# Latent attention's preparation put in another order, and the turn of the side bank between the maxima

## The chip, the cores and the metric

One core of one Trainium2 chip. The metric is the device time of one execution in microseconds (us); three runs were timed and one more execution was profiled. Engines are called as the profile calls them: PE (TensorE's matmuls), PEld (its weight loads), DVE (VectorE), ACT (ScalarE), POOL (GpSimd), SP (SyncE, which only issues DMAs here).

## The reference

Eight batches of 256 tokens of width 256 go through eight sublayers, in float32, each `x = x + f(layernorm(x))`. The order is latent attention, ternary linear, gated delta attention, ternary linear, latent attention with other weights, and then feed-forward, rotary attention, feed-forward. The change touches the two latent attentions and the closing three sublayers. A latent attention is, cut to what matters:

```python
q  = rmsnorm(x @ Wq_a) @ Wq_b              # 192 wide, to 16 heads of 128 + 64
kv = rmsnorm(x @ Wkv_a) @ Wkv_b            # 64 wide, to 16 heads of keys 128 + values 128
k_rot = rope(x @ Wk_rope); q_rot = rope(q_rot)
p = softmax(where(causal, (q_pass @ k_pass.T + q_rot @ k_rot.T) / sqrt(192), lowest))
o = (p @ v).reshape(B, T, H * 128) @ Wo
```

The ternary linear is `x @ w_ste.T + bias`. Feed-forward and rotary attention both hold a causal attention with 16 heads of width 16; the feed-forward's gate is modulated by `0.1 * tanh(attn @ A) * (h @ A) @ B`.

## The kernel before

Activations of all batches stay in SBUF. The program is a chain of blocks; within a block each engine runs a queue written out by hand, and semaphores order the engines (a `Signal` counts up by a fixed number per batch). Blocks in order: loads, `mla_sublayer` (latent attention, call 0), `delta_sublayer`, `mla_sublayer` (call 1), `small_stream` (the closing three sublayers as one stream).

**The loop of latent attention** (L872 on PE, L925 on VectorE, L973 on ScalarE, L1013 on POOL) runs over 64 pairs of heads, n = 0 to 63, eight pairs (p = 0 to 7) to a batch. In pair n PE does, in this order: scores of both heads of n (L718, L720), the query projection of pair n + 2 (L679, L680), probabilities times values of pair n - 1 (L787, L791), the output projection of pair n - 2 (L811), then a piece of preparation, and the transposes of the probabilities of n (L751, L756). VectorE: the masked maxima of both heads (L186), the scaled product oT of pair n - 2 (L800), which empties the first half of bank 6, the rope products of pair n + 2 (L686, L692), the reciprocal (L770). POOL: the rotary sum of pair n + 2 (L702) and the spread of the reciprocals (L775). ScalarE: exponentials (L739), a copy of queries (L708), copies of transposed probabilities (L765). PE's L787 of pair n - 1 waits for VectorE's oT of pair n - 2.

**The preparation** of the next batch is laid between: statistics of the layer norm on VectorE at p = 0 and the power on POOL; its normalisation (`ln_normalize_dve`, L172) at p = 1, then four transposes of it on PE (L196, `prep_early_pe`); the latent projection (L612) with ScalarE's copies and sums of squares (L629 to L635) at p = 2 and 3; at p = 4 `prep_rms_dve` (L557, L560), `prep_latent_pool` (L581 to L594: the rotary products of the keys, then the inverse rms, which needs ms_eps of L560) and `prep_norm_dve` (L568, L571: the norms of both tiles of 128 tokens); at p = 5 `prep_late_pe` (L643 to L650, six transposes; the last two wait for ScalarE's copy of the first four), `prep_late_act` and `prep_late_dve` (values, L665). The ternary sublayer of another batch goes through the same pieces at p = 5 (statistics), 6 (normalisation L172, transposes L196) and 7 (projection L449, addition L458), in thirteen of the sixteen batches. The last batch of a call has no preparation.

**The closing stream** runs over 96 slots of four heads. In slot s PE does scores (L2336), probabilities times values of s - 1 into bank 7 (L2389, L2393), feed-forward projections (L2461), a side job in bank 7 (token transposes L196, query and key projections L2204, or values L2181), the transposes of the probabilities (L2363), then L2469 and L2501. VectorE: eight masked maxima, two for each of the four heads (L186, `max_dve`), then `oT_dve`: the turn of bank 7 (L2404), reciprocal, scaling, and in every second slot the second turn (L2419). The side job may write bank 7 only when it is turned; the modulation (L2438) at a batch's first slot waits for L2419.

## Time and profile before

| | us |
|---|---|
| median of three runs | 3618.64 |
| lowest, highest | 3610.35, 3619.70 |
| the profiled execution | 3609.97 |
| its span, first to last instruction | 3608.2 |
| PE busy, DVE busy, ACT busy, POOL busy | 3313.0, 2425.1, 1959.2, 817.1 |
| granted TensorE clock, mean of the span | 0.957 |

The profiled execution is 0.24% below the median and next to the lowest run. A busy time is the union of an engine's instructions; PE's includes matmuls that run at the lower clock level, so a low granted clock hides as busy time. The page gives the busy share in 40 slices of the span; latent attention is in slices 1 to 6 and 24 to 29, the stream in the last eleven.

### The profile page before, as it was taken

The numbers are of one execution on the slowest core, as the hardware profiler recorded it, in microseconds if no ns is written. First come the engines' busy times: TensorE is split into PE (matmuls) and PEld (weight loads), VectorE is DVE, ScalarE is ACT, GpSimd is POOL, SyncE is SP. The second block draws the span as 40 slices with busy tenths as digits, with TensorE's granted clock in tenths as the row PEclk, the third lists the DMA queues.
The fourth block names the chain that finished last, engine by engine and source line by source line (L and its number), as shares of the span: only waits on it lengthen the run. The fifth ranks groups of instructions, "written<-read, shape, count | busy, mean of one in ns | idle before, by whom it ended". The sixth has DMA issues, their size and how long they took to land. (4 is left out here: it accounts for less than half of the span.)

```text
span 3608.2 us, 89141 instructions
## 1 busy us (share of the span) xinstructions
PE 3313.0 (92%) x34218; PEld 2701.3 (75%) x34218; DVE 2425.1 (67%) x7923; ACT 1959.2 (54%) x4767; POOL 817.1 (23%) x827
## 2 busy tenths in 40 slices
PE   6888896999999999999999868888979999999999
PEld 5676774888888888888888756766757777777787
DVE  4665654778777777777777535565656767777764
ACT  2444453666666666666666524454545555555553
POOL 2322221222222222222222222222210111111100
PEclk8998997999999999999999978898989999999999
DMA  5000000000000000000000040000000000000000
GB/s 223 1 1 1 1 1 18 14 20 20 20 20 20 20 20 20 20 20 20 20 20 20 8 151 1 1 1 1 1 1 1 1 1 1 1 1 7 4 7 10
DMA packets 51336, 66.83 MB, mean 19 GB/s; under 512 B 4962, under 2 KB 40290, under 8 KB 49378
## 3 DMA queue, kind: packets, MB, share of 16 engines
q1 hardware_dynamic: 50914, 61.13, 5.3%
q8 instruction: 274, 4.49, 0.5%
q14 instruction: 148, 1.21, 0.1%
HBM read 58.56 MB, written 2.56 MB: 17 GB/s over the span
## 5 line engine op out<-in xcount | busy, mean ns | idle before, releaser
L1286 DVE SCALAR_TENSOR_TENSOR d_acc<-d_raw,d_taps,d_acc 128x255 f32<-128x255 f32 (+2 forms) x1152 | 642.9, 599 | 146.2 <-ACT d_raw L1276 132.6
L2355 ACT ACTIVATE s_probs<-s_probs,s_nmax 128x128 f32<-128x128 f32 (+1 forms) x768 | 280.7, 443 | 187.9 <-DVE s_nmax L186 187.3
L1511 ACT COPY d_power<-bank 128x768 f32<-128x768 f32 x320 | 259.0, 809 | 218.7 <-PE bank L1504 218.7
L702 POOL TENSOR_TENSOR a_q<-a_rope 64x512 f32<-64x512 f32 x128 | 164.0, 1281 | 738.7 <-DVE a_rope L692 384.7
L186 DVE CUSTOM_DVE_ANT_0 a_area<-bank,mask 128x128 f32<-128x128 f32 (+1 forms) x512 | 160.3, 355 | 241.8 <-PE bank L720 239.4
L739 ACT ACTIVATE a_area<-a_area,a_nmax 128x128 f32<-128x128 f32 (+1 forms) x512 | 226.6, 444 | 165.2 <-DVE a_nmax L186 164.1
L1274 ACT ACTIVATE d_acc<-bank,d_tap_bias,d_taps 128x256 f32<-128x256 f32 x384 | 196.0, 561 | 166.5 <-PE bank L1255 158.7
L186 DVE CUSTOM_DVE_ANT_0 s_probs<-bank,mask 128x128 f32<-128x128 f32 (+1 forms) x768 | 220.9, 353 | 61.7 <-PE bank L2336 60.6
L765 ACT COPY a_area<-bank 128x512 f32<-128x512 f32 (+1 forms) x260 | 140.1, 578 | 138.7 <-PE bank L756 138.1
L2377 DVE COPY s_probsT<-bank 128x384 f32<-128x384 f32 x192 | 106.0, 555 | 119.9 <-PE bank L2363 117.7
L692 DVE TENSOR_TENSOR a_rope<-bank,a_sinT 32x512 f32<-32x512 f32 x256 | 177.4, 693 | 5.6
L720 PE MATMUL bank<-a_latT,a_q 128*128 128x256 f32 x512 | 172.2, 422 | 0.0
L1314 POOL TENSOR_TENSOR d_qT<-d_acc,d_sigm 128x512 f32<-128x512 f32 x64 | 84.4, 1319 | 370.5 <-ACT d_sigm L1296 370.5
L679 PE MATMUL bank<-a_latT,a_wq 128*128 128x256 f32 x512 | 154.8, 384 | 7.9 <-DVE a_rope L692 4.5
L1654 POOL TENSOR_TENSOR d_o_rs<-d_o_var,minus_half 128x4 f32<-128x4 f32 x64 | 69.5, 1087 | 402.4 <-DVE d_o_var L1648 402.4
L811 PE MATMUL bank<-a_w_out,a_area 128*128 128x256 f32 x512 | 154.3, 426 | 1.9 <-DVE a_area L800 1.9
L680 PE MATMUL bank<-a_qT,a_wq 128*128 128x256 f32 x512 | 153.1, 381 | 0.0
L2363 PE MATMUL bank<-ident,s_probs 128*128 128x128 f32 x1152 | 147.9, 276 | 4.6 <-ACT s_probs L2355 1.8
L686 DVE TENSOR_TENSOR a_rope<-bank,a_cosT 64x512 f32<-64x512 f32 x128 | 88.9, 695 | 92.3 <-PE bank L680 91.8
L2363 PEld LDWEIGHTS bank<-ident,s_probs 128*128 128x128 f32 x1152 | 131.7, 142 | 19.0 <-ACT s_probs L2355 11.3
L2461 PE MATMUL bank<-s_xT,m_w_up 128*128 128x256 f32 x512 | 140.5, 397 | 4.1 <-DVE s_hidden L2492 4.1
L180 POOL TENSOR_TENSOR rstd<-var_eps,minus_half 128x2 f32<-128x2 f32 x64 | 46.0, 718 | 432.8 <-DVE var_eps L162 428.0
(267 smaller groups left out, 8783.3 us busy)
## 6 DMA issues: line engine op xcount, KB each, us to landing
d_alpha<-d_alpha_rows SPq DMA_DIRECT2D x64, 256.0 KB, 3.5
d_g_decay<-d_running_rows SPq DMA_DIRECT2D x32, 258.0 KB, 3.4
a_w_o<-in_a_w_o SPq DMA_DIRECT2D x2, 2048.0 KB, 16.5
a_area<-in_a_q_nope SPq DMA_DIRECT2D x2, 1536.0 KB, 8.2
x<-in_x SPq DMA_DIRECT2D x8, 256.0 KB, 16.3
d_wk<-in_d_wk SPq DMA_DIRECT2D x1, 2048.0 KB
d_wq<-in_d_wq SPq DMA_DIRECT2D x1, 2048.0 KB
d_wv<-in_d_wv SPq DMA_DIRECT2D x1, 2048.0 KB
```

Of the source, the lines that this page charges most:

```text
L186: return core.nc.vector.tensor_tensor_reduce(out=out, in0=scores, in1=core.mask[:, blocks], scale=-1.0, scalar=HIGHEST, op0=ALU.add, op1=A ...
L679: nc.tensor.matmul(out, wq0[:, h], latT[:, it % 2, 0], start=True, stop=False)
L692: last = nc.vector.tensor_tensor(rope2[other], b_q[rows, :].rearrange("p (j t) -> p j t", j=2), sinT[rows].rearrange("p (j t) -> p j t", j ...
L702: nc.gpsimd.tensor_tensor(q[CL:P, n % 2], rope1[CL:P], rope2[CL:P], ALU.add)\
L720: nc.tensor.matmul(out[:, P:3 * P], q[:, n % 2, j, P:T], keys, start=False, stop=True, skip_group_check=True).then_inc(g.scores_in_psum.se ...
L739: last = nc.scalar.activation(own, own, ACT.Exp, scale=-1.0, bias=nmax[:, h % AHEAD, t:t + 1], accum_out=sums[:, n % 2, j, t:t + 1])
L811: last = nc.tensor.matmul(b_y[:, t * D:(t + 1) * D], oT[:, n % 2, t * P:(t + 1) * P], w_out[:, p], start=(p == 0 and t == 0), stop=(p == P ...
L1274: nc.scalar.activation(acc[:, r % 3, j], b_proj[:, j * T:(j + 1) * T], ACT.Identity, scale=taps[:, r // 2, h, 3:4], bias=tap_bias[:, r // ...
L1286: last = nc.vector.scalar_tensor_tensor(out=acc[:, r % 3, j, d:T], in0=raw[:, r % 2, j, 0:T - d], scalar=taps[:, r // 2, h, 3 - d:4 - d], ...
L1511: nc.scalar.copy(power[:], b_step[:, :, 0:3 * P]).then_inc(g.step_out, 1)
L2355: last = nc.scalar.activation(own, own, ACT.Exp, scale=-1.0, bias=nmax[:, s % 2, t, i:i + 1])
L2363: last = nc.tensor.transpose(heads[:, i, n * P:(n + 1) * P], probs[:, s % 2, i, n * P:(n + 1) * P], core.ident[:])
```

## The change

In `mla_sublayer`: the last two transposes of `prep_late_pe` go to the unused half of bank 6 (`b_qT1`), so they don't wait for ScalarE's copy; the norms are split by tile, tile 0 at the end of pair 4 and tile 1 in pair 5 before the values copy; `prep_rms_dve` and the late part stand ahead of the rope; the normalisations at p = 1 and p = 6 stand right behind the maxima, ahead of oT; on POOL the latent part at p = 4 stands ahead of the rotary sum of pair n + 2, which now also waits for the inverse rms. In `small_stream`: the turn (`turn_dve`) is taken out of `oT_dve` and stands between the maxima of heads one and two and of three and four. No instruction is added or removed. The diff:

```diff
--- before.py
+++ after.py
@@ -385,6 +385,7 @@
         b_prep, b_q, b_s, b_pT, b_o, b_y = (core.bank[0], core.bank[1], core.bank[3:5],
                                             [core.bank[5], core.bank[2]], core.bank[6],
                                             core.bank[7])
+        b_qT1 = b_o[0:QL1, T:2 * T]
         PAIRS_ALL = NB * PAIRS
 
 
@@ -560,11 +561,12 @@
             nc.vector.tensor_scalar(ms_eps[:], ms[:], 1e-6, None, ALU.add)\
                 .then_inc(g.ms_eps_ready.sem, 1)
 
-        def prep_norm_dve(dve, it):
-            dve.wait_ge(*g.rms_ready(it, 1))
-            dve.wait_ge(*g.latT_in_psum(it, 0))
-            dve.wait_ge(*g.v_ready(it, 0))
-            for t in range(NT):
+        def prep_norm_dve(dve, it, tiles):
+            for t in tiles:
+                if t == 0:
+                    dve.wait_ge(*g.rms_ready(it, 1))
+                    dve.wait_ge(*g.latT_in_psum(it, 0))
+                    dve.wait_ge(*g.v_ready(it, 0))
                 nc.vector.scalar_tensor_tensor(
                     out=q_tok[:, t], in0=lat[:, t, 0:QL], scalar=inv_rms[:, t, 0:1],
                     in1=norm_w[:, 0:QL], op0=ALU.mult, op1=ALU.mult).then_inc(g.norm_ready.sem, 1)
@@ -639,14 +641,14 @@
             pe.wait_ge(*g.norm_ready(it, 2 * NT))
             pe.wait_ge(*g.kpe_ready(it, 1))
             pe.wait_ge(*g.lat_ready(it, NT))
+            pe.wait_ge(*g.latT_ready(it, 0))
             for t in range(NT):
                 nc.tensor.transpose(b_prep[:, t * P:(t + 1) * P], q_tok[:, t, 0:P], core.ident[:])
                 last = nc.tensor.transpose(b_prep[:, T + t * P:T + (t + 1) * P], k_tok[:, t],
                                            core.ident[:])
             last.then_inc(g.latT_in_psum.sem, 1)
-            pe.wait_ge(*g.latT_ready(it, 1))
             for t in range(NT):
-                last = nc.tensor.transpose(b_prep[0:QL1, t * P:(t + 1) * P], q_tok[:, t, P:QL],
+                last = nc.tensor.transpose(b_qT1[:, t * P:(t + 1) * P], q_tok[:, t, P:QL],
                                            core.ident[:])
             last.then_inc(g.latT_in_psum.sem, 1)
 
@@ -657,7 +659,7 @@
             nc.scalar.copy(latT[:, half].rearrange("p a t -> p (a t)"), b_prep[:, :])\
                 .then_inc(g.latT_ready.sem, 1)
             act.wait_ge(*g.latT_in_psum(it, 2))
-            nc.scalar.copy(qT1[0:QL1, half], b_prep[0:QL1, 0:T]).then_inc(g.latT_ready.sem, 1)
+            nc.scalar.copy(qT1[0:QL1, half], b_qT1).then_inc(g.latT_ready.sem, 1)
 
         def prep_late_dve(dve, it):
             dve.wait_ge(*g.norm_ready(it, 2 * NT))
@@ -910,7 +912,7 @@
                 if after_attention:
                     ternary_row_sum_dve(dve)
                 prep_rms_dve(dve, -1)
-                prep_norm_dve(dve, -1)
+                prep_norm_dve(dve, -1, range(NT))
                 prep_late_dve(dve, -1)
                 if after_attention:
                     ternary_weight_dve(dve)
@@ -927,28 +929,30 @@
                     if n < PAIRS_ALL:
                         max_dve(dve, n, 0)
                         max_dve(dve, n, 1)
+                    if it + 1 < NB and p == 1:
+                        ln_normalize_dve(core, dve, mla_at(it + 1), it + 1)
+                    if ternary_in(it) is not None and p == 6:
+                        ln_normalize_dve(core, dve, ternary_at(ternary_in(it)), ternary_in(it))
                     if n > 1:
                         oT_dve(dve, n - 2)
+                    if it + 1 < NB:
+                        if p == 4:
+                            prep_rms_dve(dve, it)
+                        if p == 5:
+                            prep_norm_dve(dve, it, [1])
+                            prep_late_dve(dve, it)
                     if n + 2 < PAIRS_ALL:
                         rope_dve(dve, n + 2)
+                    if n < PAIRS_ALL:
+                        recip_dve(dve, n)
                     if it + 1 < NB:
                         if p == 0:
                             mla_stats_dve(dve, it + 1)
-                        if p == 1:
-                            ln_normalize_dve(core, dve, mla_at(it + 1), it + 1)
                         if p == 4:
-                            prep_rms_dve(dve, it)
-                        if p == 5:
-                            prep_late_dve(dve, it)
-                    if n < PAIRS_ALL:
-                        recip_dve(dve, n)
-                    if it + 1 < NB and p == 4:
-                        prep_norm_dve(dve, it)
+                            prep_norm_dve(dve, it, [0])
                     if ternary_in(it) is not None:
                         if p == 5:
                             ternary_stats_dve(dve, ternary_in(it))
-                        if p == 6:
-                            ln_normalize_dve(core, dve, ternary_at(ternary_in(it)), ternary_in(it))
                         if p == 7:
                             ternary_add_dve(dve, ternary_in(it))
                     if n > 1 and p == 1:
@@ -1013,14 +1017,14 @@
                 for n in range(PAIRS_ALL):
                     it, p = n // PAIRS, n % PAIRS
                     pool.wait_ge(*g.q_rope_ready(0, min(n + 2, PAIRS_ALL)))
+                    if it + 1 < NB and p == 4:
+                        prep_latent_pool(pool, it)
+                        pool.wait_ge(*g.rms_ready(it, 1))
                     if n + 2 < PAIRS_ALL:
                         rope_pool(pool, n + 2)
                         pool.wait_ge(*g.q_rope_ready(0, n + 3))
-                    if it + 1 < NB:
-                        if p == 0:
-                            ln_rstd_pool(core, pool, mla_at(it + 1))
-                        if p == 4:
-                            prep_latent_pool(pool, it)
+                    if it + 1 < NB and p == 0:
+                        ln_rstd_pool(core, pool, mla_at(it + 1))
                     if ternary_in(it) is not None:
                         if p == 5:
                             ln_rstd_pool(core, pool, ternary_at(ternary_in(it)))
@@ -2339,10 +2343,10 @@
                                             skip_group_check=True)
             last.then_inc(g.scores_in_psum, 1)
 
-        def max_dve(dve, s):
+        def max_dve(dve, s, members_):
             need(dve, g.scores_in_psum, s + 1)
             need(dve, g.probsT_in_psum, GS * (s - 1))
-            for i in range(GS):
+            for i in members_:
                 for t, cols in ((0, slice(0, P)), (1, slice(P, 3 * P))):
                     masked_max_dve(core, probs[:, s % 2, i, cols], heads[:, i, cols], cols,
                                    nmax[:, s % 2, t, i:i + 1]).then_inc(g.max_ready, 1)
@@ -2395,13 +2399,15 @@
                                         tile_position=(0, 32 * i), skip_group_check=True)
             last.then_inc(g.pv_in_psum, 1)
 
-        def oT_dve(dve, s):
-
-            j, k = s // SETS, s % SETS
-            cols = slice(HD * (k % 2), HD * (k % 2 + 1))
+        def turn_dve(dve, s):
             need(dve, g.pv_in_psum, s + 1)
             need(dve, g.scaled, s)
             nc.vector.transpose(turned[:], b_side[:, 0:T]).then_inc(g.turned, 1)
+
+        def oT_dve(dve, s):
+
+            j, k = s // SETS, s % SETS
+            cols = slice(HD * (k % 2), HD * (k % 2 + 1))
             need(dve, g.turned, s + 1)
             nc.vector.reciprocal(recip[:], blocks(turned[:])[:, :, HD:HD + 1])\
                 .then_inc(g.recip_ready, 1)
@@ -2571,7 +2577,11 @@
                     for i, step in steps_at(s - 1):
                         hidden_dve(dve, i, step)
                     if 0 <= s < SLOTS:
-                        max_dve(dve, s)
+                        max_dve(dve, s, range(GS // 2))
+                    if 0 < s <= SLOTS:
+                        turn_dve(dve, s - 1)
+                    if 0 <= s < SLOTS:
+                        max_dve(dve, s, range(GS // 2, GS))
                     if k == 0 and is_ffn(j + 1):
                         var2_dve(dve, j + 1)
                     if 0 < s <= SLOTS:
```

## Rows read from the trace of the kernel before

**Rows 1.** Windows, loops and stream: busy us of PE, PEld, DVE, ACT, POOL; clock; DMA.
```profile
54.57:552.27 497.70, 435.46 (x2446) 349.39 (x2444) 301.71 (x991) 245.28 (x790) 140.17 (x181) 0.92 0.02 6
2133.05:2637.67 504.62, 443.61 (x2442) 355.62 (x2440) 298.55 (x983) 246.96 (x790) 138.74 (x180) 0.91 0.00 1
2672.65:3608.17 935.52, 887.64 (x6861) 697.50 (x6860) 635.50 (x2637) 506.54 (x1360) 94.85 (x91) 0.99 0.01 4
```
**Rows 2.** Waits of PE, first call's loop: us in total, times, longest.
```profile
PE bank L196 <- DVE xn L172: 29.5, 13, 4.2
PE bank L787 <- DVE a_area L800: 26.8, 8, 3.6
```
**Rows 3.** Windows: fourth batch by pair, p = 1 to 7; last, another batch's pair 7.
```profile
247.71:256.58 8.87, 6.80 (x42) 5.44 (x41) 7.22 (x23) 4.21 (x13) 3.89 (x5) 0.96 0.00 0
256.58:264.94 8.36, 8.36 (x41) 6.50 (x41) 3.88 (x13) 3.73 (x13) 1.38 (x2) 0.84 0.01 2
264.94:272.01 7.07, 7.07 (x43) 5.48 (x41) 3.88 (x13) 4.52 (x17) 1.67 (x3) 1.00 0.00 0
272.01:277.78 5.77, 5.77 (x38) 4.71 (x37) 4.05 (x15) 4.05 (x16) 0.44 (x2) 1.00 0.00 0
277.78:291.83 14.05, 9.75 (x45) 7.58 (x43) 6.37 (x25) 4.70 (x14) 6.28 (x10) 0.69 0.01 1
291.83:302.05 10.22, 8.08 (x42) 6.60 (x42) 5.45 (x15) 4.13 (x12) 2.98 (x3) 0.83 0.00 1
302.05:310.31 8.26, 8.26 (x45) 6.86 (x45) 4.55 (x14) 3.20 (x11) 1.66 (x2) 0.91 0.00 1
169.88:177.38 7.50, 7.50 (x47) 6.23 (x46) 4.56 (x14) 3.46 (x12) 1.98 (x3) 1.00 0.00 0
```
**Rows 4.** Timeline (start, us, instruction, idle before), VectorE and PE behind scores at 264.94.
```profile
265.80 0.29 DVE L186 CUSTOM_DVE_ANT_0 a_area<-bank,mask 128x128 f32<-128x128 f32 x1 [2.35 <-PE bank L720]
...
267.02 0.42 DVE L800 TENSOR_TENSOR a_area<-bank,a_area 128x256 f32<-128x256 f32 x1
...
268.08 0.44 PE L787 MATMUL bank<-a_area,a_values 128*64 128x256 f32 x2
268.18 0.69 DVE L686 TENSOR_TENSOR a_rope<-bank,a_cosT 64x512 f32<-64x512 f32 x1 [0.75 <-PE bank L680]
```
**Rows 5.** Timeline, end of pair 4 and pair 5: POOL's chain and VectorE.
```profile
277.40 0.16 DVE L557 TENSOR_TENSOR a_ms<-a_sumsq,a_ms_scale 128x4 f32<-128x4 f32 x1
...
278.98 0.45 POOL L581 TENSOR_TENSOR a_k_t<-a_lat,a_cos_tok 128x128 f32<-128x128 f32 x1
...
281.43 0.20 POOL L594 TENSOR_TENSOR a_inv_rms<-a_inv_rms,a_q_scale 128x4 f32<-128x4 f32 x1
281.67 0.51 DVE L568 SCALAR_TENSOR_TENSOR a_q_tok<-a_lat,a_inv_rms,a_norm_w 128x192 f32<-128x192 f32 x1 [3.81 <-POOL a_inv_rms L594]
...
282.92 0.29 DVE L186 CUSTOM_DVE_ANT_0 a_area<-bank,mask 128x128 f32<-128x128 f32 x1
```
**Rows 6.** Timeline: normalisation beside POOL at p = 1, and in the stream.
```profile
253.11 1.68 DVE L172 TENSOR_SCALAR xn<-x,mean_var,rstd 128x256 f32<-128x256 f32 x2
253.33 1.31 POOL L702 TENSOR_TENSOR a_q<-a_rope 64x512 f32<-64x512 f32 x1 [3.28 <-DVE a_rope L692]
...
2925.08 0.73 DVE L172 TENSOR_SCALAR xn<-x,mean_var,rstd 128x256 f32<-128x256 f32 x2
```
**Rows 7.** Closing stream: costliest groups of the page, timeline, and a wait of PE.
```profile
L2355 ACT ACTIVATE s_probs<-s_probs,s_nmax 128x128 f32<-128x128 f32 (+1 forms) x768 | 280.7, 443 | 187.9 <-DVE s_nmax L186 187.3
L186 DVE CUSTOM_DVE_ANT_0 s_probs<-bank,mask 128x128 f32<-128x128 f32 (+1 forms) x768 | 220.9, 353 | 61.7 <-PE bank L2336 60.6
...
2901.69 0.40 PE L2393 MATMUL bank<-s_probsT,s_v 128*32 128x128 f32 x8
2903.60 0.45 DVE L2404 STREAM_TRANSPOSE s_turned<-bank 128x256 f32<-128x256 f32 x1
...
PE bank L196 <- DVE s_turned L2404: 10.7, 8, 2.0
```

More of the change, by code:

```diff
@@ L2396, in pv_pe @@
             last.then_inc(g.pv_in_psum, 1)
+        def turn_dve(dve, s):
+            need(dve, g.pv_in_psum, s + 1)
+            need(dve, g.scaled, s)
+            nc.vector.transpose(turned[:], b_side[:, 0:T]).then_inc(g.turned, 1)
         def oT_dve(dve, s):
@@ L2401, in oT_dve @@
             cols = slice(HD * (k % 2), HD * (k % 2 + 1))
-            need(dve, g.pv_in_psum, s + 1)
-            need(dve, g.scaled, s)
-            nc.vector.transpose(turned[:], b_side[:, 0:T]).then_inc(g.turned, 1)
             need(dve, g.turned, s + 1)
```

## The prediction

> **What bounds the kernel now.** I first read the busy time of the stages that the change touches [rows 1]; delta attention between them stays as it is. In the two calls of latent attention (64 head pairs each) PE is busy 435 of 498 us and 444 of 505 us, and its granted clock is only 0.92 and 0.91: some 60 us idle in each, and besides that work done at the lower of the two clock levels (1.2 instead of 2.4 GHz). In the closing stream it is 888 of 936 us at 0.99. So PE is the bound in all three, and the only time to be had is where PE stands still or runs slow.
>
> Who stops it is in the waits of PE in the first call [rows 2]: 29.5 us in its transposes of the normalised tokens (L196, for VectorE's L172) and 26.8 us before probabilities times values (L787, for VectorE's L800). Where in a batch this lies shows when one batch is cut at the first scores matmul of each pair [rows 3]. An ordinary pair (p = 4) takes 5.77 us with PE busy for all of it. Pairs 2 and 3 carry the latent projection: 7.07 at full clock. Pair 7 carries the ternary projection: 7.50 at full clock. Pair 1 takes 8.87 with 2.07 idle, pair 5 takes 14.05 with 4.3 idle and clock 0.69, pair 6 takes 10.22 with 2.1 idle and clock 0.83; and pairs 2 and 7, which don't idle, take 8.36 and 8.26 since the clock is still low behind the stall before them (0.84, 0.91). All the excess is in and behind pairs 1, 5 and 6, the three that the change rearranges.
>
> **Pair 5, the large stall.** Before, VectorE ends pair 4 with prep_norm_dve and sits 3.81 us for POOL's inverse rms; POOL starts its latent products (L581) only at 278.98, when the rotary sum of pair 6 is out of its way, and needs until 281.63 [rows 5]. The maxima of pair 5 stand behind that wait, the output product (L800) behind the maxima, and PE behind L800. Pair 5's scores began at 277.78, so by the ordinary pair [rows 4] its maxima were due at 278.64 (0.86 after its scores) and came at 282.92.
> After, POOL does the latent part first in pair 4. It is free early: ScalarE makes the second latent tile in pair 3, ahead of that pair's transposed copies, so by pair 4's scores at 272.01, and the whole chain from L581 to the end of L594 is 2.65 us long [rows 5]. Its middle waits for ms_eps, which VectorE now makes ahead of the rope: the ordinary pair leaves VectorE 0.75 us idle there [rows 4], and the two small instructions (the first takes 0.16 [rows 5]) need some 0.35, so they cost nothing (without that cover, 0.35 x 14 = 5 us). They come behind L800, 2.5 us after pair 4's scores, from 274.5 to 274.85. Were the whole chain behind them, inv_rms would be there at 277.5; the three latent products don't need ms_eps, so I take 276.3. The rope of pair 6 ends on VectorE at 277.4, so neither POOL's rotary sum, now queued behind the wait for rms, nor the norm waits. What stood in the stall is gone.
> What is late next: tile 0's two norms lie between 277.5 and 278.6; four norms took 1.25 us, from 281.67 to 282.92 [rows 5], so two take 0.63. The second meets POOL's rotary sum (1.31 us) and may be held by it, as the second normalisation is in [rows 6]; then it ends at about 279.1 and the maxima of pair 5 are 0.45 late. L787 starts 3.14 after the scores and L800 is done 2.50 after them [rows 4], some 0.5 us of slack with the signal's way, so 0.45 still fits. Tile 1's norms (0.63) and the values copy (0.3, an estimate from the norms) follow L800, which leaves 0.74 free before the rope, and push the rope of pair 7 by up to 0.6 us; nobody needs that rope for more than a pair. PE then has six transposes more than an ordinary pair. Eight matmuls of 256 columns make pair 7 longer by 7.50 - 5.77 = 1.73 [rows 3], 0.216 each, so a transpose of 128 columns is 0.11 and six are 0.65; their wait for ScalarE in between is gone because the second group goes to the free half of bank 6. Pair 5: 5.77 + 0.65 = 6.42.
>
> **Pairs 1 and 6, the normalisation.** Before, it comes behind the rope, takes 1.68 us for two instructions and meets POOL's rotary sum, which runs from 253.33; in the closing stream the same two take 0.73 with POOL idle [rows 6]. So the second is held until POOL is through (254.64; it ends at 254.79). After, it stands right behind the maxima, where POOL has nothing but the last 0.1 us of a spread to do: I take 0.75 to 0.9 us.
> The Trainium skill (SBUF — State Buffer, Who interferes with whom) has this as a rule: a VectorE instruction in a 2-port mode, or one with two SBUF inputs against a POOL instruction that reads SBUF, takes the shared port pair exclusively, and who starts first blocks the other. By that rule the normalisation is freed, and the second norm of tile 0 is held in its place; the trace agrees in [rows 6]. Were POOL no matter, the two would cost 1.68 wherever they stand, and the time would be that of the rival "held" below.
> The price is that L800 and the rope move back by that time. Of the 0.75 to 0.9 the slack of 0.5 before L787 takes most; with VectorE 0.2 to 0.4 late into both pairs (pair 0's statistics, pair 5's tail) a PE stall of 0.55 in pair 1 and 0.5 in pair 6 is left in place of 2.07 and 2.1. With four transposes (0.43): pair 1 6.75, pair 6 6.70. Bounds of the stall: 0 (everything in the slack) and 1.5 (the instructions still held). VectorE's own work in pair 1 was 7.22 us [rows 3], of which 1.68 - 0.73 = 0.95 was being held: 6.3, still under PE's 6.75, but near.
>
> **The clock.** The short stalls decide whether the clock falls too. In the batch shown it is 0.96 and then 0.84 around the 2.07 us stall of pair 1, 0.69 in pair 5, and 1.00 in pairs without a stall [rows 3]. The closing stream keeps 0.99 although PE waits 8 times for the turn, 1.3 us each on average [rows 1, 7]. I take the clock as full for the whole loop after the change, for pairs 2 and 7 too.
>
> **The sum for latent attention.** A batch with a ternary step: 5.77 + 6.75 + 7.07 + 7.07 + 5.77 + 6.42 + 6.70 + 7.50 = 53.05. Each call has six of these, one without the ternary step (pairs 6 and 7 at 5.77: 50.39), and the last batch, which prepares nothing and has seven periods up to the window's end, 7 x 5.77 and at most one ternary normalisation: 41. Together 409.7 us. Before, the two windows are 497.70 and 504.62 [rows 1]. Saved: 88.0 + 94.9 = 182.9 us. The preparation ahead of each loop loses one short wait of PE between two groups of transposes, beside the weights' staging; bounded by the 2.07 us of the longer wait in pair 1 it is 0 to -4 for both calls, and I take 0.
>
> **The closing stream.** The turn (L2404, 0.45 us) now comes after four of eight maxima, 1.15 us sooner: 220.9 us of maxima in 96 slots are 2.30 a slot, half of it 1.15. It needs the product of values, whose last matmuls (L2393) end at 2902.09, while half of the maxima are done at 2903.60 - 1.15 = 2902.45 [rows 7]; so in an ordinary slot it does not wait. In 8 slots PE waited for the turn with the token transposes (L196), 10.7 us [rows 7], of which at most 1.15 each can go, less where PE then meets the last head's exponentials: about 0.85 x 8 = 7. A few other projections wait for the same signal; they are in the bound. The wait of the modulation (L2438) for `oT` stays: that chain still ends behind all eight maxima. Heads three and four get their maxima 0.45 later, but ScalarE needs 280.7/384 = 0.73 us a head against VectorE's 0.58 and is behind by then, so 0.1 us reaches the exponentials; most slots give PE other work there. Net -7; bounds -11 and +10 (0.1 in each of 96 slots).
>
> Sum: 3609.97 (the profiled execution; span 3608.2) - 182.9 - 7 = 3420. The median of the runs is 3618.64, the fastest 3610.35, so the profile stands at the low end. I give **3420**.
>
> **Rivals.**
> Clock: the remaining half-microsecond stalls still make the clock fall. Price from [rows 3]: pair 1 without a fall would be 5.77 + 0.43 + 2.07 = 8.27 and took 8.87, pair 2 took 8.36 for 7.07; 1.9 us in all, for 14 pairs 1 and 12 pairs 6: 49 us, 3469. For it: 2.07 was enough. Against: the stream. Chance 0.14.
> Held: POOL still runs beside the normalisation, which keeps its 1.68 and stalls PE 0.95 more, 26 times: 25 us, 3445. For it: POOL's spread or power can slip there when VectorE enters the pair late. Against: both are shorter than the rotary sum. Chance 0.10.
> Half: the order in pair 4 doesn't do what it says: ms_eps or the latent tile comes so late that POOL's rotary sum and tile 0 wait for it, and half the gain of the loops is lost, 3420 + 91 = 3511. It decides if inv_rms is later than 277.5, 1.2 us after my estimate. Chance 0.04.
> Slower: the turn in the middle of the maxima waits for the values' product and puts its 0.45 us into the path of every slot, 96 x 0.45 = 43 us, while in the loops the stall only moves from L568 to the rope's consumers: 3610 + 43 = 3653. It decides from the point where the loops give back under 43 of 183 us. For it: VectorE does the same work in the same time. Against: 0.4 us between the product's end and the turn. Chance 0.02.
> My forecast has 0.69, the last 0.01 is for no change. Its own spread is 3400 (no stalls left, stream at -11) to 3440. The range takes in the clock rival: 3395 to 3470. A measurement can tell 0.3%, 11 us. Faster by over that 0.97, within 0.01, slower 0.02.
>
> **What would show it.** Cut at the first scores matmul, pair 5 near 6.4, pairs 1 and 6 near 6.7, pairs 2 and 7 at 7.07 and 7.50, granted clock near 1.00 in both loops; the wait of L568 for POOL gone; L787's wait for L800 left with many entries of half a microsecond; L172 at 0.75 to 0.9 for two. In the stream, L196's waits for the turn (10.7 us) down to some 4 us, L2438's for `oT` as before. Wrong would be: clock under 0.97 in the loops, POOL's rotary sum of pair 6 starting over 0.5 us behind the rope, or exponentials turning up among PE's waits in the stream.

## The result, and the profile after

The changed kernel takes **3391.14 us** (median of four runs, 3390.88 to 3391.84); the kernel before, timed with it, 3618.28 (3610.35 to 3619.70). The ratio is 0.9377, with a 95% interval from 0.9361 to 0.9393: 6.2% faster. The forecast was 3420, the range 3395 to 3470. The direction and the size of the large part (the loops) were right, and the time lies 29 us below the forecast and 4 below the range.

The profiled execution took 3391.38 us with a span of 3389.6, against 3609.97 and 3608.2 before. From the top of the profile's page, the busy time of each engine and the granted clock in 40 slices:

```profile
PE 3221.4 (95%) x34218; PEld 2645.8 (78%) x34218; DVE 2403.6 (71%) x7923; ACT 1954.6 (58%) x4767; POOL 820.5 (24%) x827
...
PEclk8999989999999999999999979999989999999999
```

PE is busy 92 us less with the same 34218 instructions (3313.0 before); the mean granted clock went from 0.957 to 0.980. The windows of the two loops of latent attention and of the stream, answering to [rows 1] (us, busy us of PE, PEld, DVE, ACT, POOL, clock, DMA share, GB/s):

```profile
51.99:458.36 406.37, 399.61 (x2446) 324.83 (x2445) 295.59 (x991) 239.90 (x790) 141.96 (x182) 1.00 0.03 10
2034.91:2439.71 404.80, 399.16 (x2442) 324.41 (x2441) 293.48 (x983) 240.78 (x790) 140.07 (x180) 1.00 0.01 1
2474.84:3389.60 914.76, 878.60 (x6861) 699.14 (x6860) 625.08 (x2637) 512.51 (x1360) 94.95 (x91) 1.00 0.01 4
```

The loops gave 91.3 and 99.8 us, 191.1 together (forecast 182.9). The stream gave 20.8 (forecast 7, bound 11). The three stretches outside them gave 2.6 (up to the first scores), 4.2 (between the calls) and nothing (0.1 the other way) before the stream. That is the whole difference of 218.6.

One batch, cut at the first scores matmul of each pair from p = 0 to 7, answering to [rows 3]:

```profile
259.35:265.12 5.77, 5.77 (x38) 4.71 (x37) 4.10 (x15) 3.40 (x12) 0.15 (x1) 1.00 0.01 3
265.12:271.70 6.58, 6.28 (x42) 5.24 (x41) 6.20 (x22) 3.84 (x13) 2.99 (x4) 1.00 0.00 0
271.70:278.77 7.07, 7.07 (x43) 5.48 (x41) 3.88 (x13) 3.79 (x13) 2.25 (x4) 1.00 0.00 0
278.77:285.83 7.06, 7.06 (x42) 5.47 (x41) 3.88 (x13) 4.50 (x17) 1.67 (x3) 1.00 0.01 2
285.83:291.61 5.78, 5.78 (x39) 4.72 (x38) 4.33 (x16) 4.06 (x16) 3.03 (x7) 1.00 0.01 1
291.61:298.04 6.43, 6.43 (x45) 5.37 (x44) 6.26 (x20) 4.06 (x14) 1.98 (x3) 1.00 0.00 0
298.04:304.42 6.38, 6.27 (x42) 5.23 (x41) 5.31 (x20) 3.92 (x13) 2.74 (x4) 1.00 0.00 0
304.42:311.93 7.51, 7.51 (x47) 6.25 (x46) 4.56 (x14) 3.47 (x12) 3.79 (x5) 1.00 0.02 4
```

PE stands still only in pairs 1 and 6, 0.30 and 0.11 us, and the clock is full in all eight. Pair 5 fell from 14.05 to 6.43 us. In the timeline of its VectorE and POOL (start, duration, instruction, idle before and releaser) the chain that was the stall now lies inside pair 4, which began at 285.83:

```profile
288.43 0.17 DVE L561 TENSOR_SCALAR a_ms_eps<-a_ms 128x4 f32<-128x4 f32 x1
...
291.32 0.39 DVE L570 SCALAR_TENSOR_TENSOR a_q_tok<-a_lat,a_inv_rms,a_norm_w 128x192 f32<-128x192 f32 x1
291.63 1.30 DVE L573 SCALAR_TENSOR_TENSOR a_k_tok<-a_lat,a_inv_rms,a_norm_w 128x64 f32<-128x64 f32 x1
292.96 0.29 DVE L186 CUSTOM_DVE_ANT_0 a_area<-bank,mask 128x128 f32<-128x128 f32 x1
...
294.74 0.28 DVE L573 SCALAR_TENSOR_TENSOR a_k_tok<-a_lat,a_inv_rms,a_norm_w 128x64 f32<-128x64 f32 x1
```

```profile
286.21 0.46 POOL L583 TENSOR_TENSOR a_k_t<-a_lat,a_cos_tok 128x128 f32<-128x128 f32 x1
...
289.78 0.20 POOL L596 TENSOR_TENSOR a_inv_rms<-a_inv_rms,a_q_scale 128x4 f32<-128x4 f32 x1
291.43 1.42 POOL L704 TENSOR_TENSOR a_q<-a_rope 64x512 f32<-64x512 f32 x1 [1.45 <-DVE a_recip L772]
```

POOL starts the latent products 0.38 us after the scores of pair 4 and has the inverse rms at 289.98, long before VectorE asks for it at 291.32. The second norm of tile 0 (L573 at 291.63) takes 1.30 us beside POOL's rotary sum and 0.28 alone, for tile 1 at 294.74. The maxima of pair 5 begin 1.35 us after its scores, 0.49 late against the 0.86 of an ordinary pair [rows 4], and PE loses nothing by it.

### The profile page after: what moved, and what is told of

It is laid out like the page before. It is cut to its first block and busy times, and to the rows that moved or that the text cites. A ratio compares the mean times of both kernels' runs of the same rounds, so it can differ in the third digit from the quotient of the medians.

```text
span 3389.6 us, 89251 instructions
## 1 busy us (share of the span) xinstructions
PE 3221.4 (95%) x34218; PEld 2645.8 (78%) x34218; DVE 2403.6 (71%) x7923; ACT 1954.6 (58%) x4767; POOL 820.5 (24%) x827
## 5 line engine op out<-in xcount | busy, mean ns | idle before, releaser
L2359 ACT ACTIVATE s_probs<-s_probs,s_nmax 128x128 f32<-128x128 f32 (+1 forms) x768 | 287.9, 447 | 184.4 <-DVE s_nmax L186 183.6
L2367 PE MATMUL bank<-ident,s_probs 128*128 128x128 f32 x1152 | 148.4, 275 | 6.3 <-ACT s_probs L2359 3.6
L722 PE MATMUL bank<-a_latT,a_q 128*128 128x256 f32 x512 | 152.9, 380 | 0.0
L2367 PEld LDWEIGHTS bank<-ident,s_probs 128*128 128x128 f32 x1152 | 130.5, 141 | 21.9 <-ACT s_probs L2359 14.4
L813 PE MATMUL bank<-a_w_out,a_area 128*128 128x256 f32 x512 | 144.7, 405 | 1.9 <-DVE a_area L802 1.9
L1508 PE MATMUL bank<-d_power 64*64 64x64 f32 x4096 | 142.2, 217 | 0.0
```

The costliest lines, as they stand in the source:

```text
L722: nc.tensor.matmul(out[:, P:3 * P], q[:, n % 2, j, P:T], keys, start=False, stop=True, skip_group_check=True).then_inc(g.scores_in_psum.se ...
L2359: last = nc.scalar.activation(own, own, ACT.Exp, scale=-1.0, bias=nmax[:, s % 2, t, i:i + 1])
L2367: last = nc.tensor.transpose(heads[:, i, n * P:(n + 1) * P], probs[:, s % 2, i, n * P:(n + 1) * P], core.ident[:])
```

## What was held against what

The stream had given three times its term. The first expectations hold two readings of that against each other. **M** is the forecast's own: only the time in which PE's matmuls stood still for the turn can be won, 7 to 11 us, and the rest of what was gained comes out of the latent part. **W** was formed after the result, from the trace of the kernel before: in 32 more slots only PE's weight load came late for the turn, without a gap between the matmuls, and each of these hides some 0.35 us. A third reading is that the stream gains by a state which the loops leave behind, the phase of the clock or of the queues. The other questions were how the loops' gain divides (H, in these expectations, is the forecast's account that POOL's rotary sum holds the second instruction of the normalisation), and what the turn's place does to the two other users of VectorE in a slot, the exponentials and the modulation.

The runs were made in three series, 1 to 4, 5 to 8 and 9 to 12, on three chips, each with the kernel before beside them (3616.20, 3618.00 and 3617.94 us). Unless said otherwise, a median is compared with the changed kernel's 3389.61 us in the second series, or with the kernel before in the same series.

## Experiments

**1. The stream's change alone, on the kernel before.** Only `turn_dve` is taken out of `oT_dve`:

```diff
-                        max_dve(dve, s)
+                        max_dve(dve, s, range(GS // 2))
+                    if 0 < s <= SLOTS:
+                        turn_dve(dve, s - 1)
+                    if 0 <= s < SLOTS:
+                        max_dve(dve, s, range(GS // 2, GS))
```

> The kernel before with the split of the turn alone. Theory W (hidden weight loads): in the trace of before PE's weight loads wait for the turn 32.9 us in 42 slots, while its matmuls wait only 13.2 us in 10; the other 32 slots hide some 0.35 us each, because the first weight load after the wait no longer overlaps the matmul in front of it. So the stream gets shorter by 20 to 21 us (935.5 to about 915) and the time with it. Rival M (matmul gaps alone, as predicted): 7 to 11 us, and the rest of what the changed kernel gained came out of the latent part. Everything ahead of the stream as before within 1 us or a step of the clock.

3594.09 us (3586.04 to 3595.05), ratio 0.9929 [0.9915, 0.9944], 22 us less; in its profile the stream takes 912.6 instead of 935.5. The whole of the stream's gain comes from the turn, with the loops as they were. M with its 7 to 11 us is out, and so is a state left by the loops. The profile also shows how much the loops scatter by themselves: the first takes 505.5 us here and 497.7 in the kernel before, with the same code.

**2. The loops' change alone**: the changed kernel with the stream's edit undone.

> The changed kernel without the split of the turn: only the latent attention's part. Theory W: 3391 + 20.5 = 3412, the two loops at 406.4 and 404.8 us as in the changed kernel, the stream at 935. Rival M: 3391 + 7 to 11 = 3398 to 3402.

3415.90 us (3408.59 to 3416.83), ratio 0.9437 [0.9423, 0.9451]; loops 406.3 and 404.9, stream 935.9. 200 us here and 22 there are 222, and both together gave 227 (first comparison) and 228 (second series): they add up within the scatter.

**3. The normalisation back behind the rope**, all else as changed:

```diff
-                    if it + 1 < NB and p == 1:
-                        ln_normalize_dve(core, dve, mla_at(it + 1), it + 1)
-                    if ternary_in(it) is not None and p == 6:
-                        ln_normalize_dve(core, dve, ternary_at(ternary_in(it)), ternary_in(it))
                     if n > 1:
                         oT_dve(dve, n - 2)
...
                         rope_dve(dve, n + 2)
+                    if it + 1 < NB and p == 1:
+                        ln_normalize_dve(core, dve, mla_at(it + 1), it + 1)
                     if n < PAIRS_ALL:
                         recip_dve(dve, n)
+                    if ternary_in(it) is not None and p == 6:
+                        ln_normalize_dve(core, dve, ternary_at(ternary_in(it)), ternary_in(it))
```

> The changed kernel with the normalisations of pairs 1 and 6 put back behind the rope. Theory H (the second of the two instructions is held by POOL's rotary sum): both take 1.68 us again for two, PE waits 2.07 us in 26 pairs, and a pair 1 without a fall of the clock takes 8.5 (6.58 now): 26 x 1.9 = 50 us; with the clock falling behind each of them, 3.4 each: 88 us. I expect 3445 to 3480, with granted clock under 0.97 in the loops. Rival: with the large stall of pair 5 gone, PE's short stalls are absorbed and it costs under 25 us.

3471.01 us (3469.07 to 3476.76), ratio 0.9598 [0.9582, 0.9614]; some 80 us more than the changed kernel, loops 446.9 and 443.2. PE waits 87.8 us in 31 for L172 again, as in the kernel before. A pair 1 with the pair 2 behind it, as windows:

```profile
287.45:297.03 9.58, 7.50 (x42) 6.15 (x41) 7.15 (x22) 4.34 (x13) 3.90 (x5) 0.88 0.00 0
297.03:304.69 7.66, 7.66 (x42) 5.98 (x42) 3.89 (x13) 3.48 (x12) 1.38 (x2) 0.92 0.00 0
```

The stall of 2.1 us is back, and with it the fall of the clock (0.88, 0.92) in or behind 11 of the 14 pairs 1, but only 4 of the 12 pairs 6 with the same stall. This also gives a number that the forecast lacked: where the clock doesn't fall, pair 1 with its stall takes 8.50 us (calculated there as 8.27).

**4. POOL's latent part back behind the rotary sum**, all else as changed:

```diff
-                    if it + 1 < NB and p == 4:
-                        prep_latent_pool(pool, it)
-                        pool.wait_ge(*g.rms_ready(it, 1))
                     if n + 2 < PAIRS_ALL:
                         rope_pool(pool, n + 2)
                         pool.wait_ge(*g.q_rope_ready(0, n + 3))
+                    if it + 1 < NB and p == 4:
+                        prep_latent_pool(pool, it)
```

> The changed kernel with POOL's latent part put back behind the rotary sum of pair 6. Theory: VectorE's norm of tile 0 waits for POOL until 4 us behind the rope's end again, pair 5 goes from 6.43 to 12 or 13 us and pair 6 gets a lower clock: 14 x (6 + 1.5) = 105 us, 3490 to 3505. Rival (the split of the norms by tile and the early ms_eps do most of it): under 50 us.

3451.51 us (3449.84 to 3452.95), ratio 0.9540 [0.9526, 0.9554]: 62 us more, neither the 100 to 115 of the theory nor the under 50 of its rival. Pair 5 takes 9.6 to 12.6 us, most often 11.3. A pair 5 and the pair 6 behind it:

```profile
308.78:320.06 11.28, 8.18 (x45) 6.93 (x44) 6.52 (x24) 4.61 (x14) 5.72 (x9) 0.85 0.00 0
320.06:326.42 6.36, 6.27 (x42) 5.24 (x41) 4.53 (x15) 3.58 (x12) 1.31 (x3) 1.00 0.00 0
```

The stall is there, but shorter (PE busy 8.18 of 11.28, so 3.1 us idle for 4.3 in before), and the clock is back inside pair 5 (0.85, in before 0.69), and pair 6 pays nothing (6.36 at full clock, in before 10.22). My expectation had carried the clock's price of before [rows 3] over into a kernel that pays it less. Run 11 finds part of where it went.

**5. The changed kernel again**, as the reference of its series.

> The changed kernel itself, on the same chip as the next three, to compare them with. 3391 us, loops 406.4 and 404.8, stream 914.8.

3389.61 us (3388.60 to 3395.88), ratio 0.9369 [0.9357, 0.9382]; loops 406.3 and 404.8, stream 914.6.

**6. The normalisation one place later**, between the scaled product and the rope:

```diff
+                    if n > 1:
+                        oT_dve(dve, n - 2)
                     if it + 1 < NB and p == 1:
                         ln_normalize_dve(core, dve, mla_at(it + 1), it + 1)
                     if ternary_in(it) is not None and p == 6:
                         ln_normalize_dve(core, dve, ternary_at(ternary_in(it)), ternary_in(it))
-                    if n > 1:
-                        oT_dve(dve, n - 2)
```

> The changed kernel with the normalisations of pairs 1 and 6 between the scaled product and the rope, not ahead of the product. Theory H: it is free of POOL there too (0.73 to 0.8 us for two), and PE's wait in front of the values' product (12.1 us in 19 times) goes; pair 1 6.58 to about 6.25, pair 6 6.39 to 6.22: 13 x 0.33 + 13 x 0.18 = 6.6 us, 3384.5. Rival: the rope is 0.8 late there and POOL's rotary sum with it, which gives the gain back or more: 3391 or above.

3380.30 us (3379.76 to 3380.85), ratio 0.9340 [0.9327, 0.9353]. The loops take 402.3 and 401.4. A pair 1:

```profile
263.16:269.37 6.21, 6.21 (x43) 5.15 (x42) 5.96 (x22) 3.84 (x13) 2.62 (x4) 1.00 0.00 0
```

PE is busy throughout, and pairs 1 and 6 take 6.21 in place of 6.58 and 6.38. What the change left there was L802 coming late for L789, and it costs 0.37 and 0.17 us a pair, of which 0.30 and 0.11 were idle time of PE. The normalisation stays free of POOL here too (L172 at most 413 ns). The normalisation can wait that long: its transposes lie behind the projections of the same pair.

**7. The turn after three heads** (six of eight maxima) instead of two:

```diff
-                        max_dve(dve, s, range(GS // 2))
+                        max_dve(dve, s, range(3))
...
-                        max_dve(dve, s, range(GS // 2, GS))
+                        max_dve(dve, s, range(3, GS))
```

> The changed kernel with the turn behind the maxima of three heads instead of two, so 0.56 us later. Theory W: half of the hidden weight-load waits are back, the weight loads' wait for the turn is between 6.6 us (changed) and 32.9 (before), and the stream is 8 to 12 us longer: 923 to 927, 3400. Rival M: under 4 us.

3393.07 us (3391.06 to 3396.86), ratio 0.9377 [0.9364, 0.9389]; stream 913.4. I expected half of the gain to go, and little went. The stream's 913.4 against 914.6 flatters it: in run 5 the clock is low in slots 0 and 76 (0.76 and 0.85) and here it is full, which is worth 3.1 us. The slots in which PE's matmuls wait for the turn are 2.3 us longer together (L196's waits grow from 2.9 to 6.3 us), and all other slots 0.4 shorter, so the edit costs some 2 us. But of the 32 slots in which only the weight load had waited 30 are as short as in run 5. So their gain is not in proportion to the advance: they need the turn only some 0.35 us sooner, and 0.58 does that as well as 1.15.

**8. The whole chain up to oT between heads two and three, in the slots with k = 0**:

```diff
                         turn_dve(dve, s - 1)
+                        if k == 0:
+                            oT_dve(dve, s - 1)
...
-                    if 0 < s <= SLOTS:
+                    if 0 < s <= SLOTS and k > 0:
                         oT_dve(dve, s - 1)
```

> The changed kernel with the whole chain to oT (turn, reciprocal, scaling, second turn) between heads two and three in each item's first slot, where the modulation waits for it. Theory: that wait (L2444 for L2425, 13.4 us in 9 times) falls by the 1.15 us of the four maxima each, 9 to 10 us; the exponentials of heads three and four are 1 us later but PE has the modulation's matmuls meanwhile: 3381 to 3384. Rival: the transposes of the probabilities then wait for the last heads and take it back: 3388 to 3392.

3379.68 us (3377.39 to 3384.31), ratio 0.9341 [0.9328, 0.9354]; stream 904.9, 9.7 less. The wait of the modulation, 13.4 us in nine before this edit:

```profile
  PE bank L2444: 3.7, 5
```

What the change had left of that chain behind all maxima is worth some 8 us by its slots. That the stream lost 9.7, as much as the wait, is in part luck: eight of the nine slots with the modulation are 1.0 us shorter, slot 76 is 2.5 shorter because the clock doesn't fall in it either, and slot 48, where no modulation waits, is 1.0 longer.

**9. Both better places together** (6 and 8):

> The changed kernel with both other placements at once: the normalisation between the scaled product and the rope, and the whole chain of the turn up to oT between heads two and three in the slots with k = 0. Alone they took 9.3 and 9.9 us off. They lie in different stages, so the theory expects the sum: 3389.6 - 19 = 3370 (3367 to 3374), loops of 402.3 and 401.4 us, stream near 905. Rival: part of one gain was the phase of the clock between the stages, and the two together give under 14 us (over 3375).

3374.15 us (3373.30 to 3379.85), ratio 0.9334 [0.9320, 0.9349]. Where the edits lie, both gains are there in full:

```profile
52.19:454.58 402.39, 399.53 (x2445) 324.43 (x2444) 295.54 (x991) 239.94 (x790) 141.70 (x182) 1.00 0.03 11
2036.39:2437.75 401.36, 398.33 (x2442) 323.36 (x2440) 293.31 (x983) 240.78 (x790) 139.82 (x180) 1.00 0.01 1
2472.86:3378.06 905.20, 877.68 (x6861) 698.24 (x6860) 627.27 (x2637) 514.60 (x1360) 94.86 (x91) 1.00 0.01 4
```

3.9, 3.4 and 9.4 us less than in run 5. The median gave 15 and not 19, a little outside what was expected; by the ratios (0.9334 for 0.9369) it is 13, which would be the rival's side. That the two add up is shown by the windows and not by the times. In this profile the stretch between the calls, which no edit touches, took 1581.8 us and in that of run 5 1573.6; over all profiles here it takes 1573.6 to 1581.8. A difference of 4 us between medians is within that. This is the fastest median of the study, though its interval overlaps those of 6 and 8 alone.

**10. The turn after the first head:**

```diff
-                        max_dve(dve, s, range(GS // 2))
+                        max_dve(dve, s, range(1))
...
-                        max_dve(dve, s, range(GS // 2, GS))
+                        max_dve(dve, s, range(1, GS))
```

> The changed kernel with the turn after the first head's maxima. It is asked for 0.58 us earlier still; by the row of the product of values (end 2902.09 in the slot shown, first head's maxima done at 2901.87) it then waits some 0.2 us for the product in an ordinary slot. Theory (only the first projections of a slot care, and nearly all are already free): stream within 3 us of 914.6, at most 4 of the 9.2 + 5.3 us of weight-load waits go, time 3386 to 3392. Rival, the mechanism of the forecast's case slower: the wait of the turn stands in the path of three heads' maxima in 96 slots, 0.2 x 96 = 19 us, stream near 930, time over 3400, exponentials among PE's waits.

3396.89 us (3394.22 to 3398.53), ratio 0.9393 [0.9379, 0.9407]; stream 920.4, 5.8 longer than in run 5 and in neither case's band. The turn waits for the product of values, but 3.7 us in 7 slots and not in all 96. The price stands where the exponentials are waited for. Who waited for L2359, the exponentials' line, with the turn after three, two and one heads, one line from each kernel (us, times):

```profile
  PEld bank L2367: 11.5, 26
```

```profile
  PEld bank L2367: 14.3, 32
```

```profile
  PEld bank L2367: 23.1, 52
```

With the turn behind all four heads it is 11.3 us in 26. Every head whose maxima stand behind the turn gets its exponentials 0.45 us later. After one head ScalarE has no backlog yet (it stands still for the maxima 162 times here and 89 in run 5), the delay reaches PE's transposes and outweighs what the turn still gives. The stream takes 935.9 us with the turn behind all four heads, 913.4 behind three (3.1 of it clock, as said), 914.6 behind two and 920.4 behind one: behind two or three it makes little difference.

**11. Bank 6 alone, on the kernel before:** the second group of transposes goes to the free half of bank 6 and no longer waits for ScalarE's copy.

```diff
-            pe.wait_ge(*g.latT_ready(it, 1))
             for t in range(NT):
-                last = nc.tensor.transpose(b_prep[0:QL1, t * P:(t + 1) * P], q_tok[:, t, P:QL],
+                last = nc.tensor.transpose(b_qT1[:, t * P:(t + 1) * P], q_tok[:, t, P:QL],
```

> The kernel before with the second group of transposes (L649) in the free half of bank 6 and nothing else. In before PE and its weight loads wait 27.7 us in 32 entries for ScalarE's copy L657, two entries to each of 16 preparations, so some 0.87 us a preparation of PE's path, 12 us for the 14 that lie in the loops. Theory: faster than before by 10 to 14 us, call loops near 492 and 499. Rival: in pair 5 VectorE's late chain is the later one anyway (the wait of L787 grows by what L649 loses) and under 4 us come.

3565.81 us (3562.49 to 3569.93), ratio 0.9858 [0.9841, 0.9875]: **52 us**, where I had worked out 10 to 14. In the profiles, whose kernel before stands at the low end of its runs, it is 40: 37.8 in the loops and 2.6 up to the first scores (45.5 in the loops against run 1's profile, which has the loops of before as well). Pairs 5, 6 and 7 of a batch in the kernel before, and the same batch here:

```profile
346.16:360.20 14.04, 9.74 (x44) 7.56 (x43) 6.35 (x25) 4.70 (x14) 6.26 (x10) 0.69 0.00 0
360.20:370.42 10.22, 8.08 (x41) 6.59 (x41) 5.46 (x15) 4.08 (x12) 2.98 (x3) 0.83 0.01 3
370.42:378.63 8.21, 8.21 (x45) 6.82 (x45) 4.55 (x14) 3.15 (x11) 1.67 (x2) 0.91 0.00 0
```

```profile
336.56:349.44 12.88, 9.26 (x44) 7.44 (x43) 6.36 (x25) 4.34 (x14) 6.27 (x10) 0.73 0.00 0
349.44:358.01 8.57, 6.43 (x43) 5.07 (x41) 5.46 (x15) 3.79 (x13) 2.66 (x3) 1.00 0.00 1
358.01:365.51 7.50, 7.50 (x47) 6.23 (x45) 4.55 (x14) 3.46 (x12) 1.99 (x3) 1.00 0.01 3
```

The large stall is untouched. In pair 5 the wait for the copy (0.68 us) goes and 1.16 comes; but 1.65 comes in pair 6 and 0.71 in pair 7, where nothing was edited: the clock is back before pair 6 begins, and the stall of pair 6 (2.1 us, in both) is not followed by a low clock. This batch is one of those with the largest gains. Over the 14 batches of both loops pair 5 gives 11.7 us (as much as I had worked out), pair 6 14.8, pair 7 8.1 and the others 3.2: some two thirds of the worth of this edit lie outside pair 5, and since PE's idle time there is the same, they are clock. It is also part of why undoing POOL's order in run 4 cost less than the theory said: there the second transposes no longer wait, and the stall of pair 5 is 3.1 us, where it is 3.6 here and 4.3 in before.

**12. All four norms together** at the end of pair 4, in the changed kernel:

```diff
                         if p == 5:
-                            prep_norm_dve(dve, it, [1])
                             prep_late_dve(dve, it)
...
-                            prep_norm_dve(dve, it, [0])
+                            prep_norm_dve(dve, it, range(NT))
```

> The changed kernel with all four norms together at the end of pair 4 (tile 1's two no longer behind the scaled product of pair 5). Theory of the forecast: the maxima of pair 5 come 0.56 us later than now (two norms of 0.28), on top of 0.45, against a slack of 0.5 before the product of values: PE stalls 0.5 us more in pair 5, pair 5 at 6.9 instead of 6.43, 14 x 0.5 = 7 us slower than the changed kernel, 3396 (3393 to 3400). Rivals: the slack takes it all (within 2 us, pair 5 at 6.4), or the stall makes the clock fall (pair 5 over 7.5, over 3405).

3394.24 us (3393.79 to 3395.41), ratio 0.9387 [0.9373, 0.9401], 4.6 us more than the changed kernel; loops 410.1 and 408.5, 7.5 us more than in run 5. A pair 5:

```profile
293.66:300.66 7.00, 6.50 (x45) 5.46 (x43) 6.79 (x23) 4.06 (x14) 2.74 (x3) 1.00 0.00 0
```

7.00 against 6.43: the slack of half a microsecond ahead of L789 is real and ends where the forecast had it end, and a stall of 0.50 us leaves the clock at 1.00.

## Why the forecast was right where it was, and where it failed

**The step that failed: the stream's term.** The forecast put -7 with a bound of -11, and the stream gave 20.8. That is 14 of the 29 us by which the time was missed. The loops gave 8 more than their sum and the stretches outside 7 where 0 was put (see below); since the time is only 4 us below the range, either of these two, had it come out as forecast, would have kept it inside as well. But they are misses of size, and the stream's is one of mechanism. With -21 in the stream's place the sum would have been 3406, and a range moved with it by the same 14 us (3381 to 3456) would have held the time. The turn was asked for 1.15 us sooner, as said, and the waits of L196 fell from 10.7 to 2.9 us, as said (to some 4). The mistake was in the count: "in 8 slots PE waited for the turn", and the bound was built on those 8. Only the matmuls' waits had been read. Who waited for the turn, L2404 in the kernel before, weight loads (PEld) included (us, times):

```profile
  PEld bank L2438: 18.0, 9
  PEld bank L196: 15.9, 12
  PE bank L196: 10.7, 8
  PEld bank L2204: 9.3, 19
  PEld bank L2181: 7.7, 11
  PE bank L2181: 2.5, 2
```

The same for L2405 in the changed kernel:

```profile
  PEld bank L2444: 9.2, 4
  PEld bank L196: 5.3, 6
  PE bank L196: 2.9, 6
  PEld bank L2185: 1.1, 2
```

The weight loads of the three side jobs waited in 12 + 19 + 11 = 42 slots, their matmuls in 10. In the other 32 the weight load came late behind the turn and the matmul right with it, less than 0.1 us behind the modelled end of the matmul ahead, so that no wait of PE is listed. A slot of before in the timeline, and its like of after (the kernel before first):

```profile
2961.55 1.03 PE L2461 MATMUL bank<-s_xT,m_w_in 128*128 128x256 f32 x4
...
2962.66 1.59 PEld L2181 LDWEIGHTS bank<-m_wv,s_xT 128*128 128x128 f32 x8 [0.49 <-DVE s_turned L2404]
2962.66 1.99 PE L2181 MATMUL bank<-m_wv,s_xT 128*128 128x256 f32 x8
```

```profile
2756.66 1.03 PE L2467 MATMUL bank<-s_xT,m_w_in 128*128 128x256 f32 x4
...
2757.31 1.70 PEld L2185 LDWEIGHTS bank<-m_wv,s_xT 128*128 128x128 f32 x8
2757.53 1.89 PE L2185 MATMUL bank<-m_wv,s_xT 128*128 128x256 f32 x8
```

From the start of one matmul group to the start of the next it is 1.11 us before and 0.87 after, and the second lasts 1.99 and 1.89: 0.34 us in a slot in which no wait of PE is listed.

I matched the 95 slot periods of the two profiles (slots counted from 0) one by one; the piece behind them is the same in both. The 32 slots in which the weight load alone had waited are shorter by 0.30 to 0.41 us, **11.1 us together**: the part that was not seen. The ten in which the matmuls had waited too gave 7.7: 5.5 in the eight of L196, for which 7 was said, and 2.2 in the two of L2181. So what was priced came out near its price and inside the bound. The nine slots with the modulation gave 0.14 each (1.3 together), as their wait for oT fell from 14.7 to 13.4 us. The rest is mostly clock. Slot 28 in the kernel before, with a wait of 1.94 us and the clock at 0.88, and in the changed kernel, with a wait of 1.80 and the clock at 1.00:

```profile
2925.63:2939.99 14.36, 12.42 (x79) 9.76 (x78) 7.95 (x32) 6.17 (x18) 3.12 (x3) 0.88 0.00 1
2723.08:2735.63 12.55, 10.75 (x80) 8.52 (x79) 7.76 (x32) 6.25 (x18) 3.12 (x3) 1.00 0.01 1
```

Slot 44 is the same, and the two gave 3.4 by the clock. Slots 76 and 0, where the clock is lower after than before, took 1.5 and 0.6 back, and the others together 0.6. In run 1, where the clock falls in none of slots 28, 44 and 76, the 32 slots gave the same 11.1. It also shows in the busy time: of the 20.8 us only 11.7 were idle time of PE (47.9 to 36.2, from [rows 1] and the window above), 9.0 went out of "busy", 8.3 of them in the 32 slots. The Trainium skill (Perfetto Trace Analysis, Tensor Engine Instruction (MATMUL, LD_WEIGHTS)) says that a matmul's end in the profile is estimated rather than observed and that PE can pull weight loads ahead of matmuls in flight; this case's rows agree: after, the weight load starts at 2757.31, 0.38 us before the modelled end of the matmuls ahead. PE's gaps alone were for that reason no bound. That it is a threshold and not proportional is run 7, and that the order of the maxima has a price is run 10.

**Heads three and four 0.45 us later** was costed at 0.1 or less a slot and hidden in most. Right in size: the matmuls' waits for the exponentials grow from 1.8 us in 2 (L2363) to 3.6 in 9 (L2367) in the whole stream, and those of the weight loads, which must be read too, from 11.3 in 26 to 14.4 in 32. The bound of +10 was never near with the turn in the middle; run 10 shows where it begins.

**Pair 5** came out at 6.43 for 6.42. Its steps too: ms_eps done 2.8 us after the scores (2.8), inverse rms 4.15 after them (4.29), the second norm of tile 0 held by POOL's rotary sum, the maxima 0.49 late (0.45), nothing lost on PE. Run 12 takes the slack away and gets the stall.

**Pairs 1 and 6** were put at 6.75 and 6.70 and take 6.58 and 6.38: the stalls left cost 0.37 and 0.17 (run 6) where 0.55 and 0.5 had been said, since VectorE enters both pairs less late than assumed. L172 is freed altogether. Its durations over the whole kernel, minimum, median and maximum in ns, in the changed kernel (before, the maximum was 1357):

```profile
L172 DVE TENSOR_SCALAR xn<-x,mean_var,rstd x128: 400/408/466, 10.8 to 3270.4; 128x256 f32<-128x256 f32 x128
```

With that, the rule of the Trainium skill weighed in the forecast (SBUF — State Buffer, Who interferes with whom) held in both directions: the instruction that no longer meets POOL is short (0.47 us at most), and the norm that now meets it is held to 1.30 us. The rival "held" is out.

**The clock** was taken as full in the loops, and it is: 1.00 in every pair. The clock rival rested on pair 1's 2.07 us being enough for a fall. The stalls left inside the batches are 0.1 to 0.4 us (PE idles up to 2.0 in a pair at the two ends of a loop), and no pair shows a lower clock behind them, nor behind the 0.50 of run 12. The loops gave 8.2 us more than the sum: 0.17 and 0.32 a batch in pairs 1 and 6 make 5 to 6 of it, and the first and last batches, some of which are 1 us shorter than put in, the rest.

**The stretches outside** were taken as 0 with a bound of -4 and gave 6.7. Up to the first scores it is 2.6, and run 11, with bank 6 alone, gives the same 2.6, so it is likely that edit's: the profiles with it have their first scores at 50.5 to 52.3 us, the two without at 54.3 and 54.6. The 4.2 between the calls I can't assign: this stretch takes 1573.6 to 1581.8 us in the kernels that share its code. The forecast put no term for a stretch that is hardly edited, and it moves by up to 8 us between executions.

**What the forecast had wrong without paying for it:** it gave bank 6 no share of its own. Alone it is 52 us; in the changed kernel it may be worth only the short wait, since no stall is left to recover from. That wasn't tried, nor were the early ms_eps and the place of the late part undone by themselves, and which part of the 200 us "belongs" to which edit depends on the order in which they are made: bank 6 first 52; POOL's order last 62; the normalisation last 81; the split by tile last 5 (7.5 by the loops' windows).

## What to carry to other kernels

Where the engine that bounds is PE, read who waited for a signal with its weight loads, not its matmuls alone: a late weight load behind a matmul cost some 0.35 us a time here and left PE "busy". Price a stall with what the clock does behind it: a short wait that lies in the recovery of a long one can be worth four times its length (0.68 us of PE's idle time, 2.7 us a batch in run 11), and perhaps only itself once the long one is gone, which wasn't tried. When a step is moved ahead on a full engine, move it only as far as its consumer needs: the turn after two or three heads gave 21 to 22 us in the stream and after one 16, and the normalisation one place later gave another 9.

## What of the hardware was not expected

- A stall of the same 2.1 us was followed by a low clock in some pairs and not in others: pair 6 at 0.83 and pair 7 at 0.91 in the kernel before, 1.00 and 1.00 in run 11, and in run 3 pairs 1 of 8.50 us beside ones of 9.58. In the stream of before the clock fell behind two of three modulation waits of 1.94 us and not behind one of 2.45. What decides between them I leave open.
- VectorE's scalar_tensor_tensor of 128 x 64 from two SBUF inputs takes 0.28 us and, begun while POOL's rotary sum runs, 1.30 us, until POOL is through; POOL's instruction itself went from 1.29 (mean of 128) to 1.42 us there.
